# A Mamba mixer and its layers on one core: dt by one softplus function in two batches, nine states multiplied with C on GpSimd, sixteen slots

## The reference, cut to what matters

```python
xz = xseq @ in_proj_w.T                      # 384 -> 2 x 768
xin, z = jnp.split(xz, 2, axis=-1)
u = silu(causal_conv3(xin) + conv_b)         # depthwise, 3 taps
dbc = u @ x_proj_w.T                         # dt (24), B (16), C (16)
dt = jax.nn.softplus(dt @ dt_proj_w.T + dt_proj_b)
A = -jnp.exp(A_log)
def step(h, inp):
    dA = jnp.exp(dt_t[..., None] * A)
    h = dA * h + (dt_t * u_t)[..., None] * B_t[:, None, :]
    y = jnp.einsum('bdn,bn->bd', h, C_t)     # 16 states
...
y = (ys + u * D) * silu(z)
return y @ out_proj_w.T
```

## Time and profile before

| | |
|---|---|
| median of 3 runs | 3674.62 us (3673.96 to 3679.95) |
| span of the profiled execution | 3674.1 us |
| TensorE busy | 3352.4 us, 91% |
| VectorE busy | 3256.0 us, 89% |
| ScalarE busy | 2759.3 us, 75% |
| GpSimd busy | 2577.3 us, 70% |
| products with C on VectorE | 768 of 672 ns |
| products with C on GpSimd | 768 of 1278 ns |

### The profile page before, as it was taken

The page is one execution under the profiler, slowest core; times in us unless marked ns, Lnnn a source line. Parts: engine busy times, 40 slices in busy tenths (PEclk is TensorE's granted clock), DMA queues, the critical chain, the costliest instruction groups (busy, mean ns, idle before and its releaser), DMA issues. The chain is left out here.

```text
span 3674.1 us, 50128 instructions
## 1 busy us (share of the span) xinstructions
PE 3352.4 (91%) x16962; PEld 2370.5 (65%) x16962; DVE 3256.0 (89%) x3376; ACT 2759.3 (75%) x5350; POOL 2577.3 (70%) x2045
## 2 busy tenths in 40 slices
PE   6989989899999989899989989898889998889997
PEld 3666666666666666666666666666657776557776
DVE  3999999999999999999999999999967887876886
ACT  5888797888789788977978787888655554875553
POOL 3898988989898988989898988989921111551100
PEclk7999999999999999999999999999999999999998
DMA  3020211202020211202020210202111113641212
GB/s 134 10 92 19 92 38 65 85 18 85 19 92 19 92 47 55 84 18 85 19 98 23 83 69 33 84 19 85 63 58 35 53 53 143 236 184 40 70 36 87
DMA packets 83586, 249.89 MB, mean 68 GB/s; under 512 B 15212, under 2 KB 24044, under 8 KB 73092
## 3 DMA queue, kind: packets, MB, share of 16 engines
q1 hardware_dynamic: 82564, 245.65, 18.6%
q10 hardware_dynamic: 768, 1.05, 0.1%
HBM read 204.73 MB, written 41.95 MB: 67 GB/s over the span
## 5 line engine op out<-in xcount | busy, mean ns | idle before, releaser
L956 POOL TENSOR_TENSOR slot<-dtu,b_rep 128x512 f32<-128x512 f32 x960 | 1206.4, 1277 | 78.5 <-PE ysum L454 77.8
L966 POOL TENSOR_TENSOR slot<-slot,c_rep 128x512 f32<-128x512 f32 x768 | 974.1, 1278 | 157.3 <-ACT carry L763 92.5
L454 PE MATMUL ysum<-ident,slot 128*128 128x128 f32 x6144 | 831.4, 280 | 31.9 <-POOL slot L966 16.7
L454 PEld LDWEIGHTS ysum<-ident,slot 128*128 128x128 f32 x6144 | 725.9, 145 | 173.0 <-issue 103.1
L754 ACT ACTIVATE state<-dt,aneg 128x512 f32<-128x512 f32 x960 | 655.4, 688 | 237.9 <-DVE slot L1065 200.8
L1065 DVE TENSOR_TENSOR slot<-state,c_rep 128x512 f32<-128x512 f32 x768 | 514.3, 672 | 0.0
L572 PEld LDWEIGHTS state<-diag_b,dtu_t 128*128 128x128 f32 x3072 | 385.0, 194 | 130.3 <-issue 121.1
L572 PE MATMUL state<-diag_b,dtu_t 128*128 128x128 f32 x3072 | 422.7, 281 | 33.0 <-ACT carry L763 16.6
L745 ACT ACTIVATE slot<-dt,aneg 128x512 f32<-128x512 f32 x576 | 405.4, 711 | 23.1 <-PE ysum L454 23.0
L1057 DVE TENSOR_TENSOR_SCAN slot<-state,slot 128x512 f32<-128x512 f32 x288 | 343.3, 1209 | 44.1 <-ACT state L754 33.6
L1057 DVE TENSOR_TENSOR_SCAN slot<-state,carry,slot 128x512 f32<-128x512 f32 x288 | 360.6, 1269 | 6.3 <-POOL slot L956 3.3
(11 more groups left out here) (272 smaller groups left out, 6291.9 us busy)
## 6 DMA issues: line engine op xcount, KB each, us to landing
c_rep<-rows_of_b_and_c SPq DMA_DIRECT2D x64, 1024.0 KB, 5.1
xres_l<-between_layers SPq DMA_DIRECT2D x18, 1536.0 KB, 9.8
xn_l<-between_layers SPq DMA_DIRECT2D x13, 1536.0 KB, 7.1
b_rep<-rows_of_b_and_c SPq DMA_DIRECT2D x16, 1024.0 KB, 4.5
between_layers<-y SPq DMA_DIRECT2D x10, 1536.0 KB, 6.4
xn<-in_x SPq DMA_DIRECT2D x16, 768.0 KB, 4.5
b_rep<-rows_of_b_and_c SPq DMA_DIRECT2D x16, 768.0 KB, 4.1
xres<-in_x SPq DMA_DIRECT2D x16, 768.0 KB, 4.5
```

Source lines behind the costliest of these rows:

```text
L454: last = mm(ysum[:, cols], slot[:, (NS * k + n) % SLOTS, cols], ident[:], start=first and j == 0, stop=final, is_transpose=True, skip_grou ...
L956: tt(slot[:, q % SLOTS], dtu[:, k % 2], b_rep[:, b_row(n)], ALU.mult).then_inc(dbu_done, 1)
L966: tt(slot[:, q % SLOTS], slot[:, q % SLOTS], c_rep[:, n], ALU.mult).then_inc(pool_mult_done, 1)
```

## The change

- dt: `dt_read_tile` becomes one pass, x + b, into `dt`. `softplus` becomes one pass with the Softplus function over several tiles at once: tiles 4 and 5 in the batch of SiLUs at step 31, tiles 0 to 3 of the next chunk in that at step 80 (SOFT). It stands behind the SiLUs and ahead of the table load that ends the batch. `dt_add`, the buffer `rl` and three of its semaphores go; `dt_done` now counts ScalarE's pass.
- POOL_N has nine states: 7 leaves it, 8 and 12 come in.
- SLOTS is 16 instead of 12; the four tiles of `rl` gave the room.
- TURN_N is (11, 14) instead of (11, 13), and a number of positions move by one to three steps, the halo's terms by twelve.
- At the start, the table load that stood ahead of the first copy stands behind the first softplus. At the end, the sum of the next layer's input waits for a decay instead of dt's last sum, and uses `dt` as its buffer.

```diff
--- before.py
+++ after.py
@@ -21,37 +21,37 @@
 STEPS = KT * NS
 BC = 2 * NS
 
-SLOTS = 12
+SLOTS = 16
 BANKS = 4
 BX, BY, BZ = 0, 1, 2
 XROWS, XBC = 64, 32
 GROUP = 4
-POOL_N, POOL_LAG = (0, 1, 2, 4, 5, 7, 9, 10), 5
-PE_N, TURN_N, SCALE_AHEAD, SCALED = (5, 7, 11, 13, 14, 15), (11, 13), 5, 2
-SUM_AT = (4, 4, 8, 5, 10, 9, 10, 12, 11, 12, 15, 14, 13, 14, 15, 15)
-
-COPY_Y, TURN_Y_AT, GATED_Y_AT = 5, (29, 38, 56, 73, 81, 1), (33, 42, 60, 76, 85, 2)
+POOL_N, POOL_LAG = (0, 1, 2, 4, 5, 8, 9, 10, 12), 5
+PE_N, TURN_N, SCALE_AHEAD, SCALED = (5, 7, 11, 13, 14, 15), (11, 14), 6, 2
+SUM_AT = (4, 4, 8, 5, 10, 9, 12, 12, 11, 12, 15, 14, 13, 14, 15, 15)
+
+COPY_Y, TURN_Y_AT, GATED_Y_AT = 5, (32, 38, 56, 73, 81, 1), (33, 42, 60, 76, 89, 3)
 Y_IN = (BX, BZ, BY, BX, BX, BZ)
-OUT_AT, OUT_PER = (0, 3, 11), (3, 3, 1)
-OUT_IN, RES_AT = (BX, BY, BX), (13, 14, 22)
+OUT_AT, OUT_PER = (0, 4, 9), (3, 3, 1)
+OUT_IN, RES_AT = (BX, BY, BX), (13, 14, 24)
 LAST_OUT_IN, EARLY_OUT_AT, LATE_OUT_AT = (BX, BY, BZ), (88, 82, 84), (89, 90, 91)
 X_SUM_AT = 86
-MEAN_AT, CENTER_AT, SQUARE_AT, VAR_AT, RSTD_AT, SCALE_AT = 18, 21, 25, 25, 31, 28
+MEAN_AT, CENTER_AT, SQUARE_AT, VAR_AT, RSTD_AT, SCALE_AT = 18, 21, 27, 23, 31, 28
 GATE_AT, GATE_IN = (20, 22, 37, 49, 62, 70), (BX, BZ, BY, BX, BY, BZ)
 IN_AT, IN_IN = (28, 33, 34, 39, 45, 47), (BY, BZ, BX, BX, BY, BZ)
-CONV_IN_AT, CONV_AT = (33, 38, 41, 46, 50, 54), (31, 37, 40, 45, 50, 51)
+CONV_IN_AT, CONV_AT = (33, 38, 41, 47, 51, 55), (31, 37, 40, 45, 51, 52)
 SILU_AT = (31, 45, 57, 80)
 SILU_CONV, SILU_GATE = ((), (0, 1, 2), (3, 4, 5), ()), ((0, 1), (2,), (3,), (4, 5))
-XP_AT, XP_COPY_AT = 53, 60
+SOFT = ((4, 6), (), (), (0, 4))
+XP_AT, XP_COPY_AT = 53, 61
 DT_AT, DT_IN = (57, 59, 63, 65, 2, 18), (BX, BY, BZ, BX, BZ, BZ)
 DT_READ_AT = (63, 65, 73, 77, 9, 23)
-DT_ADD_AT = (67, 72, 77, 92, 30, 38)
 EARLY = 4
 DT_U_AT = 4
-TURN_U_AT, COPY_U_AT = (84, 13, 29, 44, 60, 75), (95, 20, 36, 48, 68, 84)
-TURN_B_AT, COPY_B_AT = 80, 90
-DIAG_AT = (91, 94, 4, 9, 2, 7)
-HALO_AT = 20
+TURN_U_AT, COPY_U_AT = (84, 11, 29, 44, 60, 75), (95, 20, 36, 48, 68, 84)
+TURN_B_AT, COPY_B_AT = 80, 91
+DIAG_AT = (91, 94, 5, 8, 3, 8)
+HALO_AT = 32
 
 
 def later(c, first=0):
@@ -170,7 +170,6 @@
 
         sq = xres
         xp = sb("xp", [P, T])
-        rl = sb("rl", [P, EARLY, T])
         dt = sb("dt", [P, KT, T])
         dtu = sb("dtu", [P, 2, T])
         dtu_t = sb("dtu_t", [P, T])
@@ -191,7 +190,7 @@
         late_y = state[:, (STEPS - 2) % BANKS]
         norm_bank = [state[:, (STEPS - BANKS + h) % BANKS] for h in range(2)]
         total_bank = state[:, (STEPS - 1) % BANKS]
-        xs, ln = rl[:, 0:2], rl[:, 2:4]
+        xs, ln = dt[:, 0:2], dt[:, 2:4]
 
         in_w_in, params_in, x_w_in, dt_w_in = sem("in_w_in"), sem("params_in"), sem("x_w_in"), sem("dt_w_in")
         out_w_in, gate_w_in = sem("out_w_in"), sem("gate_w_in")
@@ -207,7 +206,7 @@
         xp_full, xp_read, bc_stored = sem("xp_full"), sem("xp_read"), sem("bc_stored")
         b_in, c_in = ([sem(f"{name}{j}") for j in range(NS // GROUP)] for name in ("b_in", "c_in"))
         bc_seen, res_free, c_free = sem("bc_seen"), sem("res_free"), sem("c_free")
-        dt_full, dt_read, sp_exp, sp_done, dt_done = sem("dt_full"), sem("dt_read"), sem("sp_exp"), sem("sp_done"), sem("dt_done")
+        dt_full, dt_read, dt_done = sem("dt_full"), sem("dt_read"), sem("dt_done")
         dtu_done, dbu_done, pe_dbu_done = sem("dtu_done"), sem("dbu_done"), sem("pe_dbu_done")
         u_turned, u_copied, b_turned, b_copied, diag_b_set, scaled = (
             sem("u_turned"), sem("u_copied"), sem("b_turned"), sem("b_copied"), sem("diag_b_set"), sem("scaled"))
@@ -714,18 +713,11 @@
 
             def dt_read_tile(d, m):
                 act.wait_ge(dt_full, KT * d + m + 1)
-                if m < 2 and later(d):
-                    act.wait_ge(dt_done, KT * d + m - 1)
-                if m >= EARLY:
-                    act.wait_ge(dt_done, KT * d + m - EARLY + 1)
-                af(dt[:, m], pg[DT_IN[m]][:], ACT.Abs, bias=dtb[:, m:m + 1])
-                af(rl[:, m % EARLY], pg[DT_IN[m]][:], ACT.Relu, bias=dtb[:, m:m + 1]).then_inc(dt_read, 1)
-
-            def softplus(d, m):
-                act.wait_ge(dt_read, KT * d + m + 1)
-                af(dt[:, m], dt[:, m], ACT.Exp, scale=-1.0).then_inc(sp_exp, 1)
-                act.wait_ge(sp_exp, KT * d + m + 1)
-                af(dt[:, m], dt[:, m], ACT.Ln, bias=1.0).then_inc(sp_done, 1)
+                af(dt[:, m], pg[DT_IN[m]][:], ACT.Identity, bias=dtb[:, m:m + 1]).then_inc(dt_read, 1)
+
+            def softplus(d, first, end):
+                act.wait_ge(dt_read, KT * d + end)
+                af(dt[:, first:end], dt[:, first:end], ACT.Softplus).then_inc(dt_done, end - first)
 
             def gate_silu(c, k):
                 act.wait_ge(z_full, KT * c + k + 1)
@@ -866,7 +858,6 @@
                     for k in range(KT):
                         if q == DT_READ_AT[k] and (after or k >= EARLY):
                             dt_read_tile(d if k < EARLY else c, k)
-                            softplus(d if k < EARLY else c, k)
                     for k in range(KT):
                         if after and q == CONV_IN_AT[k]:
                             conv_in(d, 1 - h, k, b)
@@ -877,6 +868,8 @@
                                     conv_silu(d, 1 - h, m)
                             for k in SILU_GATE[g]:
                                 gate_silu(c, k)
+                            if SOFT[g] and (after or SOFT[g][0] >= EARLY):
+                                softplus(d if SOFT[g][0] < EARLY else c, *SOFT[g])
                             nc.scalar.preload_act_table_set("natural_log_exp_and_others")
                     if after and q == XP_COPY_AT:
                         copy_xp(d)
@@ -894,12 +887,12 @@
                     conv_in(0, 0, m, 0)
                 for m in range(g, g + 3):
                     conv_silu(0, 0, m)
-            nc.scalar.preload_act_table_set("natural_log_exp_and_others")
             copy_xp(0)
             store_bc(0, 0)
             for m in range(EARLY):
                 dt_read_tile(0, m)
-                softplus(0, m)
+            softplus(0, 0, EARLY)
+            nc.scalar.preload_act_table_set("natural_log_exp_and_others")
             copy_b(0, 0)
             for i in diag_order():
                 set_diag(0, 0, i)
@@ -932,10 +925,6 @@
             pool.wait_ge(const_step, 2)
             nc.gpsimd.sem_inc(consts, 1)
 
-            def dt_add(d, m):
-                pool.wait_ge(sp_done, KT * d + m + 1)
-                tt(dt[:, m], dt[:, m], rl[:, m % EARLY], ALU.add).then_inc(dt_done, 1)
-
             def dt_u(c, h, k):
                 pool.wait_ge(dt_done, KT * c + k + 1)
                 pool.wait_ge(u_done, KT * (c + 1))
@@ -968,7 +957,7 @@
             def sum_x():
                 pool.wait_ge(lead.x_first[0], 16)
                 pool.wait_ge(lead.x_first[1], 16)
-                pool.wait_ge(dt_done, KT * NCHUNK)
+                pool.wait_ge(exp_done, STEPS * (NCHUNK - 1) + 2 * NS)
                 by_half = "p (h s) -> p h s"
                 tt(xs, lead.xn[:, 0].rearrange(by_half, h=2), lead.xn[:, 1].rearrange(by_half, h=2), ALU.add).then_inc(lead.x_summed, 1)
                 pool.wait_ge(lead.x_summed, 1)
@@ -994,9 +983,6 @@
                         pool_times_c(b if h else b - 1, 1 - h, q - POOL_LAG + STEPS)
                     if h == 0 and q == HALO_AT:
                         halo_terms(b)
-                    for k in range(KT):
-                        if q == DT_ADD_AT[k] and (after or k >= EARLY):
-                            dt_add(c + 1 if k < EARLY else c, k)
                     if not after and q == X_SUM_AT:
                         sum_x()
                     if q % NS == DT_U_AT:
@@ -1005,8 +991,6 @@
                         elif after:
                             dt_u(c + 1, 1 - h, 0)
 
-            for m in range(EARLY):
-                dt_add(0, m)
             dt_u(0, 0, 0)
             scan(0, 0, False, True)
             for i in range(0, NCHUNK // 2 - 1):
```

## The result

The changed kernel took 3696.51 us (median of 4 runs, 3695.86 to 3698.68), the kernel before beside it 3675.8: a ratio of 1.0052, interval 1.0038 to 1.0067. It is slower by about 20 us (21 by the medians, 19 by the ratio); I had forecast 33 us faster. The span of the profiled execution went from 3674.1 to 3694.1 us.

A forecast was written before the change was run, and what follows sets the result against it. VectorE was taken to set the pace for over half a chunk, TensorE beside it elsewhere. 2.7 - 0.9 + 0.35 - 0.2 = 2.0 us a chunk, 30 over fifteen, plus 1.5 and 2 at the ends: 3641 us, full range 3605 to 3673.

The forecast's parts named there:

- the batches: Softplus batches at steps 80 and 31: a 0.9 us stall per chunk at step 81, nothing at step 32.
- the ninth product: C for nine states on GpSimd: 2.7 us a chunk won by VectorE, bounds 1.9 and 3.5.
- slots: 16 slots instead of 12: half of VectorE's waits for GpSimd saved, 0.35 us a chunk, bounds 0 and 0.7.
- B's copy: Copy moved from step 90 to 91, keeping TensorE waiting longer: 0.2 us a chunk lost, bounds 0 and 0.7.
- What C on GpSimd frees: Six products a chunk leave VectorE at 0.59 us each: 3.5 us a chunk of its work.
- What of it counts: Of the 3.5 us, steps 0 to 21 count as nothing, 0.8; the remaining 2.7 us a chunk are won.
- a sign of being wrong: VectorE's waits for TensorE grown by more than 2 us a chunk would show the forecast wrong.
- the earlier start: Step 80's decay gets state 12's bank after its scan, not its product, so the batch starts earlier; stall 0.6 us.
- the cover: At step 31 the batch's added 2.35 us is hidden by an earlier variance; without it, up to 2.3 us lost.
- The ends: Outside the fifteen chunks: 2 us counted as won at the start, 1.5 us in the last chunk.
- The third, "slower": Rival: batches stall VectorE, 5.5 us against 2.7 won, slower once over 2.7 are uncovered; 3713 us, chance 13%.
- The second, "TensorE takes over": Rival: all 45 steps of TensorE's stretch yield nothing, leaving 1.9 us of the gain; 3666 us, chance 15%.

The follow-up runs named there:

- e1: The changed kernel with dt by Exp and Ln, tile by tile at the old places, no Softplus batches or added table loads; 3655.34 us, ratio 0.9939.
- e6: As e1, but with the old eight states on GpSimd and the old sums, keeping 16 slots and the new positions; 3673.03 us, ratio 0.9990.
- e15: As e1, with four matmuls of the output projection's second tile made twice, 3.6 us more for TensorE ahead of the mean; 3706.64 us, ratio 1.0078.
- e2: The changed kernel with all positions of the kernel before, keeping nine states on GpSimd, 16 slots and the softplus batches; 3718.82 us, ratio 1.0112.
- e16: As e1, with one matmul of each of the gate's tiles 2 to 5 made twice, at steps 37 to 70; 3675.43 us, ratio 0.9993.
- e11: As e1, with 12 slots instead of 16, nine states still on GpSimd; 3691.86 us, ratio 1.0043.
- e5: As e1, with state 6 on GpSimd in place of state 12, still nine states there; 3666.7 us, ratio 0.9972.
- e13: As e1, with eight matmuls left out of the gate projection at steps 37 to 70, 7.1 us less for TensorE; 3691.5 us, ratio 1.0040.

## Why the prediction was wrong

Two terms of the sum failed, and it took both to turn the sign. A chunk of the table gives them one by one: the batches cost 2.6 us (after against e1) where I had 0.9; the ninth product wins 1.25 (e1 against e6) where I had 2.7; all the rest wins 0.04 (e6 against the kernel before), where slots and B's copy gave 0.15. Together that is 1.3 us lost instead of 2.0 won. With only one of the two mis-sized, the sum would still have been 0.2 or 0.5 us a chunk won. What the parts are worth depends somewhat on the order in which they are taken away.

*What C on GpSimd frees.* Right: 3.5 us a chunk.

*What of it counts.* This step failed. I took steps 0 to 21 as worth nothing, 0.8 us, and all the rest, 2.7, as won. Measured are 0.7 lost ahead of the mean and 1.9 won behind it. VectorE's waits for TensorE grew by 3.4 us a chunk, from 6.1 to 9.6, and I had named a growth of over 2 as a sign of being wrong. Of that, 1.3 came with the new positions while eight states were on GpSimd (e6, 7.4), and 1.9 with the ninth product (e1, 9.3). Ahead of the mean nothing can be won: by its busy time TensorE is never idle there, neither in the kernel before nor in e6 or e1, and work added to it counts (e15). The wait at step 7, 2.4 instead of 0.9, is not the product's: with eight states at the new positions it is 2.0 (e6), while e2, with nine at the old ones, has 0.9 there and 2.4 at steps 3 and 4. The positions move it; the product adds 0.6 to the two places together. TensorE begins that part later with it, waiting 1.45 us in e1's chunk for GpSimd's last product of the tile (1.0 in the mean; in e6 it waits 0.6 there, for VectorE's). Behind the mean, 1.0 came at step 29, again with the positions (1.4 in e6; in e2 the wait there is for ScalarE), and 0.5 at step 69, with the product (0.4 in e6). I had read "VectorE hardly waits here" as "TensorE has room here"; it had little: e16 shows that even there a third or more of added work is paid.

*The batches.* The mechanism was the one I named, with the right parts (three loads, a pass of 1.915 us against my 1.89), and its size was off: 1.7 us at step 81 instead of 0.9, and 0.8 at step 32 instead of nothing. At step 81 the second half of an image came out as worked out, 0.8 against 0.6; the first half gave 2.7 against 1.2. The step that failed is the earlier start: I let it depend on the scan of state 12 alone, and it needs the carry of the state before, which waits for VectorE's product. At step 32, of the 2.35 us by which the batch grew, 1.8 show with the old positions (e2) and 0.8 with the variance asked for earlier: the cover that I took as whole was not.

By the Trainium skill, ScalarE: Activation LUTs, section What ACT_TABLE_LOAD costs, a switch of sets is 2.66 us, of which 1.28 are the load; by that figure I had estimated a stall of 2.3 us. The measured 1.7 lies between that and my 0.9, and what it has above mine is mostly the wait for the carries, 1.50 in the chunk shown. The page doesn't say on which side of the load its drain stands. No drain shows in this trace on either: the pass ends at 868.71, the load starts at 868.73 and ends at 870.01, and the next instruction starts at 870.02.

*The slots.* The saved waits for GpSimd were right in size, 0.8 at the upper bound. But I priced the slots by the waits of the kernel before, and they carried 37 us once the ninth product was there (e11).

*The ends.* The start gained 2.1 us as said; the last chunk lost 2.0 where I counted 1.5 of gain.

*The rivals.* The third, "slower", has the right sign, but not by its own terms: it needed more than 2.7 us uncovered, and 2.5 at the two steps sufficed, as the gain that they had to outweigh was 1.25 and not 2.7. The second, "TensorE takes over", had put that gain at 1.9 and is nearer there, though it too was too high. I had priced the two as alternatives, and they came together.

Open stays how much of what the ninth product frees is lost to the late start of TensorE's part: e5 shifts that product, but brings its own waits at other steps.

## What to carry to other kernels

An engine that is busy for 95% hides a second one that is busy for 93%: before a saving is counted, cut the period into stretches, and where another engine is full take the saving as zero or less, and elsewhere as a part. A function with its own table costs a load at each place where it is put into an existing batch, and a batch's length has to be set against the lead of what waits behind it, in the least favourable of the loop's variants. A buffer's worth can't be read from the waits of a kernel that doesn't yet lean on it.

## What the runs showed of the hardware

TensorE's granted clock fell after TensorE had been idle, and that turned less work into more time. In e13 TensorE waited 1.40 and 1.90 us where in e1 it waited 1.76 once; in e13 its matmuls of the input projection then took twice as long. First e13's stretches (clock third from the end) and its matmuls, then e1's:

```profile
960.00:965.00 5.00, 1.71 (x9) 1.12 (x8) 4.96 (x6) 4.97 (x8) 2.54 (x2) 0.84 0.01 2
965.00:970.00 5.00, 5.00 (x8) 1.94 (x7) 4.02 (x5) 3.71 (x7) 4.43 (x4) 0.50 0.00 0
```

```profile
961.83 0.63 PE L569 MATMUL state<-ident,dbu_t 128*128 128x128 f32 x4 [1.40 <-DVE slot L1049]
964.36 5.49 PE L362 MATMUL px<-xn,w_in 128*128 128x512 f32 x6 [1.90 <-DVE acc L1022]
```

```profile
954.10 2.84 PE L362 MATMUL px<-xn,w_in 128*128 128x512 f32 x6 [1.76 <-DVE acc L1021]
```

A granted share of 0.50 is the lower of its two levels, 1.2 GHz. The fall, 6.8 us long, stands at this place in each of e13's chunks 3 to 12 and in none of e1's. The gaps themselves did not put TensorE behind VectorE: in both kernels these matmuls start 0.14 us after the same scan (964.22 in e13, 953.96 in e1). VectorE then waited for the drive behind them, 2.92 us in this chunk and 3.1 in the mean at step 45, against 0.1 in e1:

```profile
964.22 1.27 DVE L1041 TENSOR_TENSOR_SCAN slot<-state,carry,slot 128x512 f32<-128x512 f32 x1
...
971.95 2.46 DVE L1041 TENSOR_TENSOR_SCAN state<-slot,carry,state 128x512 f32<-128x512 f32 x2 [2.92 <-PE state L572]
```

```profile
953.96 1.27 DVE L1040 TENSOR_TENSOR_SCAN slot<-state,carry,slot 128x512 f32<-128x512 f32 x1
```

Nothing else of that size differs between the two; the wait at step 69, 0.9 in e1, is gone in e13. In e1 the clock falls mostly behind the longest wait of a chunk, that for B's copy. In the chunk below TensorE waited 3.60 us, and the granted share of the 7 us from 1027 on was 0.51:

```profile
1028.48 1.09 PE L535 MATMUL pz<-ident,dtu 128*128 128x128 f32 x4 [3.60 <-ACT b_t L774]
```

```profile
1027.00:1034.00 7.00, 5.52 (x26) 5.55 (x27) 7.00 (x8) 6.24 (x15) 7.00 (x7) 0.51 0.71 200
```
